# Flamingo block with a routed feed-forward layer: where four things of the opening sit in PSUM, and where the last quarter of the routing table stands in TensorE's order

## The chip, the cores and the metric

One Trainium2 chip, one core of it. The metric is the device time of one execution in microseconds (us), as the median of several runs. A traced execution has its own time, which stands beside its span below.

## What is computed

A layer of attention over a context, and a feed-forward layer with routed and shared experts, each with a layer norm before it and a gate (a hyperbolic tangent) behind it. In short:

```python
# x (4, 512, 512), ctx (4, 512, 128)
p    = layernorm(x)
kv   = ctx @ W_k.T + b_k                       # (4, 512, 128)
out  = einsum('bij,bjd->bid', p, kv)
sim  = einsum('bid,bjd->bij', out, kv) * 512 ** -0.5
attn = softmax((sim - mean) * rsqrt(var + 1e-6) * gamma + beta)
x    = x + tanh(g_xattn) * attn

h       = layernorm(x).reshape(2048, 512)
scores  = sigmoid(h @ gate_w)                  # 32 experts
top 2 of 4 groups, then the top 4 experts of these; weights made to sum to 2.5
routed  = sum over a token's 4 experts of weight * relu(h @ Wu[e]) ** 2 @ Wd[e]
shared  = relu(h @ Wsu) ** 2 @ Wsd             # inner size 1024
out     = x + tanh(g_ffn) * (routed + shared)
```

## The kernel before

It has three stages that run into one another.

The **front** takes the four batches (512 tokens each) through the attention and, behind that, three of them through the shared expert. A batch is turned on TensorE (`ctx_t`, `kv_t`, `kv_rows`, `p_t`, `out_t`), its four tiles of scores are made (`score`), ScalarE takes their squares and exponentials (`squares`, `copied`, `exps`), VectorE scales, shifts and adds them (`scaled`, `shifted`, `added`) and makes the second norm (`x2_part`, `x2_spread`, `h_norm`). The normed rows are turned on TensorE again (`h_t`, four tiles a batch), and each is split in a high part by ScalarE (`h_t` there) and a low part by VectorE (`h_low`). A product of the shared expert is three matmuls: high by high, low by high, high by low. The shared expert goes in pieces of 128 inner columns, eight a batch, numbered 0 to 23: `up_shared(g)`, then Relu and squares (`relu2(g)`), then the low part (`low_part(g)`), then `down_shared(g)`, which adds into the banks D0 to D3. Piece 0's up product goes in two halves of columns.

The **routing** begins when all logits are there. VectorE picks the experts and the places of the tokens in the experts' lists. The table that says which token sits at which place is a product of 0/1 matrices, made in four quarters by `select(q)` on TensorE in bank T0; ScalarE makes half of the left matrices (its own `select`), VectorE the other half and the right ones. Behind the last quarter one product with zeros closes the table (semaphore `pe_ix`). VectorE then reads it and writes the indices of the gather (`idx_g`), and GpSimd gathers the rows of the first tiles from memory with an indirect DMA each (`gather`). A second small table, of the experts of each tile, is turned on TensorE in T1 (`pe_tab`).

The **routed stage** runs over 81 tiles of 128 rows. For each, TensorE turns the gathered rows (`rows`), multiplies by the expert's first matrix (`up`), turns the result (`act_t`) and multiplies by the second (`down`); ScalarE and VectorE split rows, results and weights, GpSimd gathers and scatters, SyncE loads the weights of the next expert once VectorE has split those of one before. The end adds the rows up and does the shared expert of the last batch.

What sets the order: each engine's instructions stand in an order written out by hand at the end of its block and run in that order; semaphores order the engines against each other. PSUM has eight banks here: T0, T1, U0, U1, D0 to D3. Which of them holds what is said by small functions (`sim_bank`, `h_bank`, `up_bank`, `mean_bank`), and each use of a bank waits for the last reader of what was in it. On TensorE the order around the two places is, before:

```python
h_t(0, 0); h_t(0, 1); h_t(0, 2); h_t(0, 3)
up_shared(0, 0); up_shared(0, 1)
score(2, 0); score(2, 1); logits_t(0); up_shared(1); logits(0)
score(2, 2); up_shared(2); ...
...
select(2); up_shared(22); down_shared(20)
select(3); close of the table; turn of the second table
up_shared(23); down_shared(21)
rows(0); down_shared(22); rows(1); down_shared(23); up(0)
```

Line 1801 is the helper `mm`, so nearly all matmuls of the trace have that line: they are told apart by their bank and operands. L1960 is `h_t`, L1824 `ctx_t`, L1995 `logits` on TensorE; L733 is ScalarE's `h_t`, L727 its `exps`, L719 its Relu, L747 its `logits_t`, L877 and L880 its `select`; L1085 is VectorE's `x_part`, L1108 `scaled`, L1148 `h_low`, L1156 `logits`, L1174 `low_part`, L1180 `add_shared`, L1518 the end of its small tables, L1565 `tile_square`; L614 is the gather. `PEld` rows are TensorE's loads of the stationary matrix.

Of the kernel before, what the change touches and what calls it, by code (L numbers as in the profile page):

```python
# [5 lines left out]
P = 128  # L6
N_BATCH, SEQ, H = 4, 512, 512
DC = 128
TPB = SEQ // P
# [25 lines left out]
def block_kernel(nc, x, ctx_in, g_xattn, g_ffn, w_k, b_k, ln_gamma, ln_beta,  # L35
# [6 lines left out]
    with ExitStack() as stack:  # L42
# [237 lines left out]
        def sim_bank(b, it):  # L280
            return D[it] if b < 2 else T[it % 2]

# [4 lines left out]
        def h_bank(b, it):  # L287

            return U[0] if b == 0 and it == 2 else T[0] if b == 0 and it == 3 else T[it % 2]

        def up_bank(g):

            return U[0 if g else 1]

# [357 lines left out]
        def _(ac):  # L652
# [12 lines left out]
            def ctx_t(b):  # L665

                ac.wait_ge(s["pe_ctxT"], b + 1)
                ac.activation(ctxT[:, :], T[0][:, :], ACT.Copy, accum_out=csum[:, 0:1]).then_inc(s["act_ctxT"], 1)

# [382 lines left out]
        def _(ve):  # L1052
# [165 lines left out]
            score_spread(1)  # L1218
            x_part(2, 0)
            x_part(2, 1)  # L1220
            h_low(0, 0)
            h_low(0, 1)
            h_low(0, 2)
            h_low(0, 3)
            scaled(1, 0)
            shifted(1, 0)
# [291 lines left out]
            ve.tensor_scalar(done_tab[0:1, :], cntE[0:1, :], 1.0, None, ALU.add).then_inc(s["dve_tab"], 1)  # L1518
            low_part(22)

# [5 lines left out]
            nth()  # L1526
            ve.tensor_scalar(idx_g[:, :], tsum[:, :], -1.0, 0.0, ALU.add, ALU.max).then_inc(s["dve_idx"], 1)
            ve.wait_ge(s["pe_tab"], 1)
            ve.tensor_copy(tab[0:1, :], T[1][0:1, 0:2 * P]).then_inc(s["dve_tab"], 1)  # L1529
# [269 lines left out]
        def _(pe):  # L1799
# [17 lines left out]
            def ctx_t(b):  # L1817
                pe.wait_ge(d_ctx[b], 16)
                if 0 < b < 3:
                    pe.wait_ge(s["act_kv"], b)  # L1820
                elif b == 3:
                    pe.wait_ge(s["dve_hT"], TPB + 3)
                for j in range(TPB):
                    i_ = pe.transpose(T[0][:, j * P:(j + 1) * P], ctx_b[:, j, :], ident[:, :])  # L1824
                i_.then_inc(s["pe_ctxT"], 1)

            def mean(b):

                pe.wait_ge(s["act_ctxT"], b + 1)
                if b == 1:  # L1830
                    pe.wait_ge(s["act_outT"], 1)
                elif b == 2:
                    pe.wait_ge(s["act_pT"], 2 * TPB - 1)
                elif b == 3:
                    pe.wait_ge(s["dve_lg"], 1)
                mm(mean_bank(b)[:, 0:1], wkT[:, :], csum[:, 0:1]).then_inc(s["pe_mean"], 1)
# [55 lines left out]
            def score(b, it):  # L1892
                if it == 0:
                    pe.wait_ge(s["act_outT"], b + 1)
                if b == 1:
                    pe.wait_ge(s["dve_u"], it + 1)
                elif b == 2:
                    pe.wait_ge(s["dve_hT"], TPB)
                    if it >= 2:
                        pe.wait_ge(s["act_sim"], it - 1)  # L1900
                elif b == 3:
                    pe.wait_ge(s["act_pT"], TPB * b + TPB)
                    if it >= 2:
                        pe.wait_ge(s["act_sim"], TPB + it - 1)
                mm(sim_bank(b, it)[:, :], outs_of(b)[:, it * P:(it + 1) * P], keys_of(b)).then_inc(s["pe_sim"], 1)

            def up_shared(g, part=None):

                b, k = g // SB, g % SB
                if g:  # L1910
                    if part != 1:
                        pe.wait_ge(s["act_r"], g)
                elif part == 0:
                    pe.wait_ge(s["dve_ws"], 2)
                    pe.wait_ge(s["act_outT"], 3)
                if k == 0:
# [24 lines left out]
            def h_t(b, it):  # L1941
                pe.wait_ge(s["dve_h"], TPB * b + it + 1)
                if b == 0 and it >= 2:
                    if it == 2:
                        pe.wait_ge(s["act_mean"], 5)
                    else:
                        pe.wait_ge(s["dve_hT"], 1)
                elif it >= 2:
                    if b < N_BATCH - 1:
                        pe.wait_ge(s["dve_hT"], TPB * b + it - 1)  # L1950
                    else:
                        pe.wait_ge(s["act_tT"], it - 1)
                elif b == 0:
                    pe.wait_ge(s["act_pT"], 3 * TPB)
                elif b < N_BATCH - 1:
                    pe.wait_ge(s["act_sim"], TPB * (b - 1) + it + 3)
                else:
                    pe.wait_ge(s["dve_hT"], TPB * (b - 1) + it + 3)
# [4 lines left out]
            def logits_t(b):  # L1963
# [14 lines left out]
                if b == 0:  # L1978
                    pe.wait_ge(s["d_gate"], 16 * 2)
                    pe.wait_ge(s["act_r"], 1)  # L1980
                elif b == 1:
# [62 lines left out]
            up_shared(0, 1)  # L2044
            score(2, 0)
            score(2, 1)
            logits_t(0)
            up_shared(1)
# [95 lines left out]
            up_shared(22)  # L2144
            down_shared(20)
            select(3)
            mm(table, zeros[:, :], nothing, False, True).then_inc(s["pe_ix"], 1)
            pe.wait_ge(s["dve_tabT"], 1)
            for j in range(2):
# [170 lines left out]
```

## Time and profile before

| | us |
|---|---|
| median of 3 runs | 553.31 |
| lowest and highest run | 552.16, 555.45 |
| the profiled execution, its own time | 557.28 |
| its span | 555.4 |
| TensorE busy | 538.7 (97%) |
| VectorE busy | 412.7 (74%) |
| ScalarE busy | 336.2 (61%) |
| GpSimd busy | 197.7 (36%) |

The page cuts the span into 40 slices (13.9 us each) and gives the busy share of each engine in tenths. TensorE shows a 9 in all but the first, the third and the last slice, and its granted clock is at full speed throughout (2.4 GHz). VectorE shows a 9 in the four slices from 28 to 83 us. A row of a timeline reads: start, how long, engine, line, operation, output and inputs, shapes, how many in a row, and in brackets how long the engine had been idle before it and what ended that. Neighbouring rows of one engine overlap by some 0.1 to 0.2 us, since the end of an instruction is its last write; the start of the next is the better mark.

### The profile page before, as it was taken

The page shows a single profiled execution, that of the slowest core. Times are in us where ns is not written, and L with a number is a line of the kernel's source. Part 1 is how long each engine was busy: PE and PEld are TensorE (multiplying, and loading weights), DVE is VectorE, ACT ScalarE, POOL GpSimd, SP SyncE. Part 2 cuts the span into 40 slices and gives each one's busy share as a digit, 9 for nine tenths or more (in the row PEclk, how much of TensorE's full clock was granted, in tenths as well). Part 3 has the DMA queues.
Part 4 walks back from the last instruction along what each step waited for, and adds up shares of the span by engine and source line. Part 5 has one row for each costly group of instructions (what it writes and reads, how often), then busy time and mean ns, then how long its engine had stood idle before and what let it go on. Part 6 is the DMA issues. An engine that isn't in the chain of part 4 may idle for free.

```text
span 555.4 us, 11126 instructions
## 1 busy us (share of the span) xinstructions
PE 538.7 (97%) x3090; PEld 436.7 (79%) x3091; DVE 412.7 (74%) x906; ACT 336.2 (61%) x669; POOL 197.7 (36%) x194
## 2 busy tenths in 40 slices
PE   7989999999999999999999999999999999999997
PEld 5546776777888878999999888888898888897553
DVE  4799995595979948676779696775766665667997
ACT  4779573745337845677778676765766666663210
POOL 2110000000000044565667575676556655532000
PEclk9999999999999999999999999999999999999999
DMA  8930102006000037978798788687798777899997
GB/s 311 358 110 28 41 36 76 2 1 228 1 1 1 1 90 214 369 248 267 262 317 249 266 262 261 210 297 258 234 328 257 243 238 241 268 317 370 413 414 301
DMA packets 56393, 116.48 MB, mean 210 GB/s; under 512 B 5493, under 2 KB 24054, under 8 KB 55926
## 3 DMA queue, kind: packets, MB, share of 16 engines
q1 hardware_dynamic: 43200, 72.97, 39.6%
q0 software_dynamic: 12960, 42.48, 21.4%
q8 instruction: 35, 0.57, 0.4%
q14 instruction: 48, 0.39, 0.2%
q10 hardware_dynamic: 150, 0.07, 0.0%
HBM read 85.87 MB, written 29.62 MB: 208 GB/s over the span
## 4 chain that ended last, share of the span: by engine, by line
PE 73%; DVE 10%; ACT 5%; issue 4%; another core or an unknown queue 3%; DMA 1%; ACTq 1%; DVEq 0%; POOLq 0%
PE D L1801 32%; PE U L1801 31%; PE T L2162 4%; PE D L2181 2%; PE T L1801 2%; ACT xgT_hi L914 1%; DVE X L1126 1%; DVE bst L1085 1%; DVE xgT_lo L1560 1%; DVE bst L1131 1%; DVE PS L1108 1%; DVE PS L1114 1%; ACT erel L919 1%; DMA xg<-h_rows,idx_g 1%
## 5 line engine op out<-in xcount | busy, mean ns | idle before, releaser
L621 POOL DMA_INDIRECT y_rows<-yb,idx_s x81 | 95.5, 1179 | 89.0 <-ACT yb L931 62.7
L614 POOL DMA_INDIRECT xg<-h_rows,idx_g x81 | 89.8, 1108 | 103.9 <-DVE tab L1529 73.0
L1560 DVE TENSOR_TENSOR xgT_lo<-T,xgT_hi 128x512 fp32r<-128x512 f32 x81 | 55.8, 689 | 39.8 <-ACT xgT_hi L914 33.8
L931 ACT ACTIVATE yb<-D 128x512 f32<-128x512 f32 x81 | 48.8, 602 | 46.7 <-PE D L1801 37.6
L1801 PE MATMUL U<-wu_hi,xgT_hi 128*128 x324 | 59.2, 304 | 3.8 <-DVE xgT_lo L1560 3.4
L1565 DVE SCALAR_TENSOR_TENSOR eact<-U,erel 128x256 f32<-128x256 f32 x81 | 33.9, 419 | 32.7 <-issue 16.8
L1801 PE MATMUL D<-wd_hi,eaT_hi 128*128 x162 | 57.4, 435 | 0.8 <-DVE eaT_lo L1570 0.8
L919 ACT ACTIVATE erel<-U 128x256 f32<-128x256 f32 x81 | 31.0, 383 | 38.3 <-remote 19.1
L914 ACT ACTIVATE xgT_hi<-T 128x512 fp32r<-128x512 f32 x81 | 48.6, 600 | 6.1 <-issue 3.4
L1801 PE MATMUL U<-wu_lo,xgT_hi 128*128 x324 | 51.9, 282 | 0.0
L1801 PE MATMUL U<-wu_hi,xgT_lo 128*128 x324 | 51.9, 282 | 0.0
L1801 PE MATMUL D<-wd_lo,eaT_hi 128*128 x162 | 50.6, 394 | 0.0
L1801 PEld LDWEIGHTS U<-wu_hi,xgT_hi 128*128 128x128 f32 x324 | 44.5, 189 | 7.6 <-issue 7.0
L1801 PE MATMUL D<-wd_hi,eaT_lo 128*128 x162 | 50.1, 391 | 0.0
L2162 PE MATMUL T<-ident,xg 128*128 128x128 f32 x324 | 48.5, 272 | 0.8 <-DMA xg<-h_rows,idx_g 0.8
L2162 PEld LDWEIGHTS T<-ident,xg 128*128 128x128 f32 x324 | 40.1, 140 | 11.4 <-DMA xg<-h_rows,idx_g 1.2
L1550 DVE TENSOR_TENSOR wu_lo<-wu,wu_hi x32 | 39.2, 1225 | 9.2 <-issue 9.1
L1801 PEld LDWEIGHTS U<-wu_hi,xgT_lo 128*128 128x128 f32 x324 | 44.4, 190 | 0.0
L1801 PEld LDWEIGHTS U<-wu_lo,xgT_hi 128*128 128x128 f32 x324 | 44.2, 188 | 0.1
L1778 DVE SCALAR_TENSOR_TENSOR X<-yg,w,X 128x512 f32<-128x512 f32 x60 | 40.7, 747 | 4.4 <-DMA yg<-y_rows 4.3
L588 POOL TENSOR_TENSOR rstd<-veps,mhalf 128x4 f32<-128x4 f32 x8 | 8.1, 1012 | 98.0 <-DVE veps L1136 75.1
L1801 PE MATMUL D<-wsd_hi,act_hi 128*128 128x512 f32 x96 | 39.4, 410 | 0.0
(261 smaller groups left out, 1140.6 us busy)
## 6 DMA issues: line engine op xcount, KB each, us to landing
wu<-in_L_ffn_Wu SPq DMA_DIRECT2D x32, 512.0 KB
wd<-in_L_ffn_Wd SPq DMA_DIRECT2D x32, 512.0 KB
yg<-y_rows SPq DMA_DIRECT2D x18, 512.0 KB, 11.2
out<-X SPq DMA_DIRECT2D x16, 256.0 KB, 6.0
X<-in_x SPq DMA_DIRECT2D x3, 1024.0 KB, 11.5
h_rows<-HR SPq DMA_DIRECT2D x3, 1024.0 KB, 4.3
yg<-y_rows SPq DMA_DIRECT2D x3, 1024.0 KB, 11.8
wsu<-in_L_ffn_Wsu SPq DMA_DIRECT2D x2, 1024.0 KB, 8.6
```

Of the source, the lines that this page charges most:

```text
L614: pool.indirect_dma_start(out=xg[:, u, :], out_offset=None, in_=h_dram[:, :], in_offset=bass.IndirectOffsetOnAxis(ap=idx_g[:, t:t + 1], ax ...
L621: pool.indirect_dma_start(out=y_dram[:, :], in_=yb[:, u, :], in_offset=None, out_offset=bass.IndirectOffsetOnAxis(ap=idx_s[:, t:t + 1], ax ...
L914: ac.activation(xgT_hi[:, t % 2, :, :], T[t % 2][:, :].rearrange("p (h n) -> p h n", h=HB), ACT.Copy)\
L919: ac.activation(erel[:, t % 2, :], U[t % 2][:, 0:INNER], ACT.Relu)\
L931: ac.activation(yb[:, t % UNROLL, :], D[2 + t % 2][:, :], ACT.Copy)\
L1550: ve.tensor_tensor(wu_parts[1][:, ds(split_at(v), W_N)], wu2[:, ds(raw_at(v), W_N)], wu_parts[0][:, ds(split_at(v), W_N)].bitcast(f32), AL ...
L1560: ve.tensor_tensor(xgT_lo[:, t % 2, :, :], T[t % 2][:, :].rearrange("p (h n) -> p h n", h=HB), xgT_hi[:, t % 2, :, :].bitcast(f32), ALU.su ...
L1565: ve.scalar_tensor_tensor(eact[:, t % 2, :], U[t % 2][:, 0:INNER], 0.0, erel[:, t % 2, :], ALU.max, ALU.mult).then_inc(s["dve_eact"], 1)
L1778: ve.scalar_tensor_tensor(X[:, t, :], row_at(t, k), w4[:, t * TOPK + k:t * TOPK + k + 1], X[:, t, :], ALU.mult, ALU.add).then_inc(s["dve_c ...
L1801: return pe.matmul(o, l, r, start=start, stop=stop)
L2162: i_ = pe.transpose(T[t % 2][:, h * P:(h + 1) * P], xg[:, t % UNROLL, h * P:(h + 1) * P], ident[:, :])
L2181: i_ = pe.transpose(D[t % 2][:, k * P:(k + 1) * P], eact[:, t % 2, k * P:(k + 1) * P], ident[:, :])
```

## The change

Banks: the last of batch 0's four turned tiles goes to U1 (it went to T0) and the up product of piece 0 to T0 (it went to U1). Batch 2's scores take T1, T0, T1, T0 (they took T0, T1, T0, T1). Batch 3's turned context goes to U1 (it went to T0). The waits follow the banks: `h_t(0, 3)` waits for ScalarE's copy of batch 2's output and no longer for the low part of tile 0; `up_shared(0, 0)` loses its wait for that copy; `score(2, 1)` waits for the Relu of piece 0, and `logits_t(0)`, which stands ahead of it now, doesn't; `h_t(1, 0)` waits for all four copies of batch 2's scores, not three; `ctx_t(3)` waits for VectorE's first `logits` and no longer for the low part of batch 1's third tile.

Orders: VectorE does the four `h_low(0, ...)` ahead of `x_part(2, 0)` and `x_part(2, 1)`. TensorE does `logits_t(0)` ahead of `score(2, 1)`, and `select(3)` with the close of the table ahead of `down_shared(20)`. VectorE does `low_part(22)` behind the indices of the gather.

```diff
         def sim_bank(b, it):
-            return D[it] if b < 2 else T[it % 2]
+            return D[it] if b < 2 else T[(it + 1) % 2] if b == 2 else T[it % 2]
+
+        def ctx_bank(b):
+
+            return U[1] if b == N_BATCH - 1 else T[0]
...
         def h_bank(b, it):
 
-            return U[0] if b == 0 and it == 2 else T[0] if b == 0 and it == 3 else T[it % 2]
+            return U[it % 2] if b == 0 and it >= 2 else T[it % 2]
 
         def up_bank(g):
 
-            return U[0 if g else 1]
+            return U[0] if g else T[0]
...
-                ac.activation(ctxT[:, :], T[0][:, :], ACT.Copy, accum_out=csum[:, 0:1]).then_inc(s["act_ctxT"], 1)
+                ac.activation(ctxT[:, :], ctx_bank(b)[:, :], ACT.Copy, accum_out=csum[:, 0:1]).then_inc(s["act_ctxT"], 1)
...
             score_spread(1)
-            x_part(2, 0)
-            x_part(2, 1)
             h_low(0, 0)
             h_low(0, 1)
             h_low(0, 2)
             h_low(0, 3)
+            x_part(2, 0)
+            x_part(2, 1)
             scaled(1, 0)
...
             ve.tensor_scalar(done_tab[0:1, :], cntE[0:1, :], 1.0, None, ALU.add).then_inc(s["dve_tab"], 1)
-            low_part(22)
 
             ve.wait_ge(s["pe_ix"], 1)
...
             ve.tensor_scalar(idx_g[:, :], tsum[:, :], -1.0, 0.0, ALU.add, ALU.max).then_inc(s["dve_idx"], 1)
+            low_part(22)
             ve.wait_ge(s["pe_tab"], 1)
...
                 elif b == 3:
-                    pe.wait_ge(s["dve_hT"], TPB + 3)
+                    pe.wait_ge(s["dve_lg"], 1)
                 for j in range(TPB):
-                    i_ = pe.transpose(T[0][:, j * P:(j + 1) * P], ctx_b[:, j, :], ident[:, :])
+                    i_ = pe.transpose(ctx_bank(b)[:, j * P:(j + 1) * P], ctx_b[:, j, :], ident[:, :])
...
                 elif b == 2:
                     pe.wait_ge(s["act_pT"], 2 * TPB - 1)
-                elif b == 3:
-                    pe.wait_ge(s["dve_lg"], 1)
                 mm(mean_bank(b)[:, 0:1], wkT[:, :], csum[:, 0:1]).then_inc(s["pe_mean"], 1)
...
                 elif b == 2:
                     pe.wait_ge(s["dve_hT"], TPB)
-                    if it >= 2:
+                    if it == 1:
+                        pe.wait_ge(s["act_r"], 1)
+                    elif it >= 2:
                         pe.wait_ge(s["act_sim"], it - 1)
...
                 elif part == 0:
                     pe.wait_ge(s["dve_ws"], 2)
-                    pe.wait_ge(s["act_outT"], 3)
...
                     else:
-                        pe.wait_ge(s["dve_hT"], 1)
+                        pe.wait_ge(s["act_outT"], 3)
...
                 elif b < N_BATCH - 1:
-                    pe.wait_ge(s["act_sim"], TPB * (b - 1) + it + 3)
+                    pe.wait_ge(s["act_sim"], TPB if b == 1 else TPB * (b - 1) + it + 3)
...
                 if b == 0:
                     pe.wait_ge(s["d_gate"], 16 * 2)
-                    pe.wait_ge(s["act_r"], 1)
...
             score(2, 0)
+            logits_t(0)
             score(2, 1)
-            logits_t(0)
             up_shared(1)
...
             up_shared(22)
-            down_shared(20)
             select(3)
             mm(table, zeros[:, :], nothing, False, True).then_inc(s["pe_ix"], 1)
+            down_shared(20)
             pe.wait_ge(s["dve_tabT"], 1)
```

## Rows read from the trace of the kernel before

**Rows 1.** The page: busy time of the engines, share of the span, instructions

```profile
PE 538.7 (97%) x3090; PEld 436.7 (79%) x3091; DVE 412.7 (74%) x906; ACT 336.2 (61%) x669; POOL 197.7 (36%) x194
```

**Rows 2.** Busy time by stretch: length, then busy us of PE, PEld, DVE, ACT, POOL

```profile
98.00:112.00 14.00, 14.00 (x68) 11.05 (x67) 7.85 (x18) 9.71 (x21) 1.01 (x1) 1.00 0.01 2
```

**Rows 3.** Timeline of TensorE, 28 to 89 us

```profile
41.59 0.63 PE L1960 MATMUL T<-ident,HR 128*128 128x128 f32 x4 [1.51 <-DVE hT_lo L1148]
42.19 0.71 PE L1801 MATMUL U<-hT_hi,wsu_hi 128*128 128x256 f32 x4
...
45.17 1.88 PE L1801 MATMUL T<-keyT,ctxT 128*128 128x512 f32 x4
...
51.73 0.60 PE L1995 MATMUL U<-ident,lgT 128*128 128x128 f32 x4
...
53.42 1.20 PE L1801 MATMUL U<-hT_hi,wsu_hi 128*128 128x512 f32 x4 [0.23 <-ACT act L719]
...
73.86 0.63 PE L1824 MATMUL T<-ident,ctx_b 128*128 128x128 f32 x4 [0.67 <-DVE hT_lo L1148]
...
88.44 3.59 PE L1801 MATMUL U<-pT,kv 128*128 128x512 f32 x8
```

**Rows 4.** Timeline of ScalarE, 39 to 54 us

```profile
39.30 1.08 ACT L733 ACTIVATE hT_hi<-T 128x512 fp32r<-128x512 f32 x2
...
45.00 0.72 ACT L727 ACTIVATE PS<-PS,nmax 128x512 f32<-128x512 f32 x1 [0.34 <-DVE nmax L1114]
...
50.60 0.59 ACT L747 ACTIVATE lgT<-U 128x512 f32<-128x512 f32 x1
...
52.78 0.59 ACT L719 ACTIVATE act<-U 128x512 f32<-128x512 f32 x1
```

**Rows 5.** Timeline of VectorE, 39 to 88 us

```profile
39.57 1.28 DVE L1085 BATCH_NORM_STATS2 bst<-X 128x6 f32<-128x512 f32 x2
40.77 1.27 DVE L1148 TENSOR_TENSOR hT_lo<-T,hT_hi 128x512 fp32r<-128x512 f32 x2
...
43.49 0.74 DVE L1108 SCALAR_TENSOR_TENSOR PS<-D,rstd,gam 128x512 f32<-128x512 f32 x1
...
87.04 0.67 DVE L1156 TENSOR_REDUCE LG<-U 128x128 f32<-128x512 f32 x1
```

**Rows 6.** The chain that ended last, 193 to 204 us: start, length, what

```profile
193.59 2.72 PE D L1801 x12
196.31 0.87 PE T L1801 x17
...
199.39 4.26 DMA xg<-h_rows,idx_g
```

**Rows 7.** Timeline of TensorE: the first gathered rows, and tile 2's up product

```profile
203.69 0.66 PE L2162 MATMUL T<-ident,xg 128*128 128x128 f32 x4 [0.82 <-DMA xg<-h_rows,idx_g]
...
214.67 0.75 PE L1801 MATMUL U<-wu_hi,xgT_hi 128*128 x4 [0.41 <-DVE xgT_lo L1560]
```

**Rows 8.** Timeline of ScalarE: the end of its last quarter of the table

```profile
191.68 1.15 ACT L880 ACTIVATE selA<-selA,onesE 128x1024 f16<-128x1024 f16 x1
```

**Rows 9.** Timeline of VectorE, 193 to 213 us

```profile
193.37 0.16 DVE L1518 TENSOR_SCALAR done_tab<-cntE 1x32 int32<-1x32 f32 x1
...
202.15 0.69 DVE L1174 TENSOR_TENSOR act_lo<-act,act_hi 128x512 fp32r<-128x512 f32 x1 [3.36 <-ACT act L723]
...
210.35 1.41 DVE L1180 SCALAR_TENSOR_TENSOR X<-D,g_tanh,X 128x512 f32<-128x512 f32 x2 [0.25 <-PE D L1801]
212.20 0.42 DVE L1565 SCALAR_TENSOR_TENSOR eact<-U,erel 128x256 f32<-128x256 f32 x1 [0.44 <-ACT erel L919]
```

**Rows 10.** Timeline of GpSimd: the second and the third gather

```profile
200.99 1.03 POOL L614 DMA_INDIRECT xg<-h_rows,idx_g  x1 [0.31 <-issue]
202.33 1.40 POOL L614 DMA_INDIRECT xg<-h_rows,idx_g  x1 [0.30 <-issue]
```

**Rows 11.** Waits of 206 to 500 us: us in total, times, longest

```profile
ACT erel L919 <- remote: 19.1, 9, 3.0
```

## The prediction

> **What bounds the kernel now.** I read the page's busy times first: TensorE works 97% of the span, no other engine over 74% [rows 1]. So a gain must come out of the 3% in which TensorE idles, and the change removes hardly any work. Next, the busy time by stretch: from about 84 us on TensorE has no idle time in the front (the stretch of 98 to 112 us stands for all up to 196 us: 14.00 of 14.00) [rows 2], so what it wins earlier it keeps, as long as the others deliver. Then TensorE's timeline, for the brackets with idle time. In the change's reach there are four: 1.51 us ahead of the last turned tile of batch 0, 0.23 us ahead of piece 2's up product, 0.67 us ahead of batch 3's turned context [rows 3], and 0.82 us ahead of the first gathered rows [rows 7]. The first, the third and the fourth are what the edits aim at. Whether each pays is read from who is last next.
>
> **Part 1, batch 0's turned tiles (28 to 54 us): worth nothing.** `h_t(0, 3)` waited for the low part of tile 0, since both had T0. TensorE had been free since 41.59 - 1.51 = 40.08 us [rows 3]. In U1 the tile waits for ScalarE's copy of batch 2's output, which ScalarE has behind it when it begins with the turned tiles at 39.30 us [rows 4], so it starts at 40.1, 1.5 us earlier. What follows is VectorE's. A high part on ScalarE takes some 0.6 us (the pair 1.08), so tile 0's is done at 39.9 [rows 4]. VectorE is free from 39.57 us, where `x_part(2, 0)` began, and does one of these steps in (40.77 - 39.57) / 2 = 0.60 us [rows 5]. In the new order it waits until 39.9, does four low parts to 42.3 and the two `x_part` to 43.5. `scaled(1, 0)` began at 43.49 before [rows 5]. VectorE trades one small wait for another and is where it was.
>
> TensorE does get ahead. The first half of piece 0's up product may start when the second low part is done, 39.9 + 1.27 = 41.2 us, and the two halves took 45.17 - 42.19 = 2.98 us [rows 3], so they end at 44.2 and not 45.17: a lead of 0.9 to 1.0 us. The second half needs the fourth low part, 39.9 + 1.8 + 0.7 = 42.4, which is in time. From there to `logits(0)` stands 51.73 - 45.17 = 6.56 us of TensorE work, whose sum the new order leaves alone, so it arrives at about 50.8. There it meets ScalarE. Its exponential of 45.00 us waited for VectorE [rows 4], which has not moved, and from there to 55 us ScalarE's timeline shows no gap. Its copy of the logits ends at 50.60 + 0.59 = 51.19, so the lead shrinks to 0.5; its Relu of piece 1 ends at 52.78 + 0.59 = 53.37, and piece 2's up product begins at 53.42 as before [rows 3, 4]. The lead is gone. The wait that the change adds, `score(2, 1)` for the Relu of piece 0, stands ahead of `up_shared(1)` and all behind it on TensorE. The Relu comes right behind that exponential: 45.00 + 0.7 + 0.6 = 46.3 us [rows 4]. Of the 6.56 us, 2.98 are piece 1's up product; of the other 3.58, all but one score (1.88 / 2 = 0.9) stand ahead of `score(2, 1)` now, so TensorE comes to it at 44.2 + 2.6 = 46.8: it costs nothing, with 0.5 us of cover. `h_t(1, 0)`, which now waits for the fourth copy of scores, waits anyway for batch 1's norm, and that stands in VectorE's order behind all of batch 1's softmax. Bounds for part 1: nothing on the low side; on the high side the lead, 1.0 us, and at the very most the whole idle time, 1.51 us. I take nothing, since the 0.23 us bracket at 53.42 [rows 3] shows who is last there.
>
> **Part 2, batch 3's context (74 us): 0.67 us.** `ctx_t(3)` waited 0.67 us for a low part on VectorE [rows 3]. In U1 it waits for VectorE's first `logits`, long past, so it starts when piece 2's down product ends, at 73.19. Late next could be three things. `kv_t(3)` still waits for the next low part (0.6 us more), but half an up product of 1.5 us stands between. ScalarE's copy and mean wait only for the context and move with it. And `out_t(3)` at 88.44 overwrites U1 and waits for VectorE's `logits(1)`, done at 87.04 + 0.67 = 87.71 [rows 3, 5]: a slack of 0.73, of which 0.67 is used up. It holds, barely. From there TensorE has no idle time and its feeders wait for it, so I count 0.67 us in full; bounds 0 and 0.67.
>
> **Part 3, the table (193 to 215 us): 0.69 us.** Before, `down_shared(20)` ran from 193.59 to 196.31 (2.72 us), the quarter and the close to 197.18 [rows 6]. Then came indices, issue and flight of the gather: 199.39 - 197.18 = 2.21, and 4.26 us [rows 6], in all 6.47 us. TensorE covered 203.69 - 0.82 - 197.18 = 5.69 of them, and idled 0.82 [rows 7]. Now the down product stands behind the close and covers as well: 5.69 + 2.72 = 8.41 against 6.47, 1.9 us to spare. The 0.82 us go. Can the quarter run that early? ScalarE has its part at 191.68 + 1.15 = 192.83 [rows 8], TensorE comes at 193.59: 0.76 to spare. VectorE is through its small tables at 193.53 [rows 9], and the table closes at 194.46. `low_part(22)` waits behind the indices; if it stood ahead, it would hold them for ScalarE's squares. Behind it wait only the copy of the second table, which TensorE turns behind the same down product as before, and `down_shared(22)`, which comes after the first rows. Behind `down_shared(20)`, nobody waits for it sooner than piece 23.
>
> What is late next is VectorE. It idles 0.25 us ahead of `add_shared` at 210.35 and 0.44 us ahead of `tile_square` at 212.20 [rows 9], both for TensorE, and tile 2's up product waits for it at 214.67 [rows 7]. It can move forward by 0.25 + 0.44 = 0.69 us and no more, so 0.69 of the 0.82 arrive. GpSimd's queue: the four gathers come 2.7 us earlier relative to TensorE, and it then waits for the second index as before. Bounds: 0.44 (if the first of the two stays) and 0.82.
>
> A third gather took 1.40 us and the second 1.03 us [rows 10]; beside the third ran a `low_part` of 0.69 us that starts at 202.15 [rows 9]. The first gather now has `low_part(22)` beside it. The Trainium skill, SBUF — State Buffer, Who interferes with whom, says that a VectorE instruction with two inputs in SBUF contends with a GpSimd instruction that reads SBUF, and that the loser stands still for the whole instruction. By the row that is 0.37 us a gather, by the rule up to 0.69; either is within the 1.9 us. It speaks against the reordering, and I put it into the chance of the third rival below, not into the sum.
>
> **Sum.** 0 + 0.67 + 0.69 = 1.36 us, 0.25%. The profiled execution took 557.28 us and would take 555.92. It lies 3.97 us above the median of 553.31; I carry the difference over: 553.31 - 1.36 = 551.95, rounded to 551.9.
>
> **Rivals.** (a) TensorE's lead of part 1 is kept, because ScalarE or VectorE move forward after all: another 1.0 us, 551.0, at most 1.51, 550.4. For it: a 1.5 us wait is really taken away. Against it: the 0.23 us bracket and the sum on VectorE. (b) Part 2 is taken back at `out_t(3)`, where 0.06 us is left, or by the next norm: only part 3 stays, 552.6. (c) The gather isn't earlier than TensorE needs it, because something else holds it (GpSimd also waits for twenty down products and for the small tables, or contention): only part 2 stays, 552.6. Against it: both conditions hold before 194 us. (d) Slower: weights in the routed stage. ScalarE waits there nine times for SyncE's word that weights have landed, 19.1 us in all, 2.1 us each, 3.0 the longest [rows 11]. Most of that is hidden behind TensorE. If earlier tiles bring one more of the mean size onto TensorE's path, 551.95 + 2.1 = 554.1, slower than before; from two on, 556.2, it is slower by over 0.5%. It decides as soon as the landings shift by more than the 1.36 us won. Against it: VectorE's splits ask for the weights, and these move forward with the tiles.
>
> **Chances.** The forecast 0.52, (a) 0.15, (b) 0.12, (c) 0.07, (d) 0.14. A measurement of this kernel can tell about 0.5%, 2.8 us, from no change, since its runs lie 3.3 us apart. Faster by more than that (below 550.5) needs the far end of (a), 0.05, or the scatter of the runs upon the forecast and (a), 0.11: 0.16. Slower by more (above 556.1) is the second half of (d), 0.07. Within: 0.77. The range reaches from 549.8, (a)'s end less scatter, to 554.8, (d) with one wait and scatter.
>
> **What would show it.** The trace after should have `ctx_t(3)` without its bracket; piece 2's up product at about 53.4 us with a short wait for the Relu (right), or a us earlier (rival a); a wait ahead of `out_t(3)` (rival b); the first gather about 2.2 us behind the close, the rows' turn without a bracket, and tile 2's up product some 1.4 us earlier than 214.67, at 213.3. If that holds and the end doesn't move, the brackets of the routed stage have grown (rival d). The forecast is wrong if TensorE waits for ScalarE at the last quarter or at `score(2, 1)`.

## The result, and the profile after

| | before | after |
|---|---|---|
| median, 22 runs each | 556.11 us | 554.62 us |
| mean of the same runs | 556.28 | 554.18 |
| the profiled execution, its own time | 557.28 | 555.18 |
| its span | 555.4 | 553.3 |

The ratio is 0.996, with a 95% interval of 0.9943 to 0.9978: the change makes the kernel faster by 1.2 to 3.2 us of 556, about 2.2, which is inside the 0.5% that was called no change. It was forecast as 1.36 us, or 0.9975. The forecast time of 551.9 us was too low by 2.7 us, nearly all of it for a reason that has nothing to do with the change: it started from the median of three runs, 553.31, and the median of 22 runs of the same kernel is 556.11.

The page of after, the span and the busy times, for rows 1:

```profile
span 553.3 us, 11125 instructions
...
PE 538.4 (97%) x3090; PEld 436.4 (79%) x3091; DVE 411.9 (74%) x906; ACT 337.0 (61%) x669; POOL 197.1 (36%) x194
```

TensorE does the same work (538.4 us against 538.7) in 2.1 us less. Lines moved by two to four: mm is L1805 now, `h_t` L1963, `logits` L1997, `ctx_t` L1828, VectorE's `h_low` L1152, its `logits` L1160, `low_part` L1178. Traces don't begin at the same point of the work: VectorE's first `h_norm` starts at 37.05 us in the trace of before, at 36.67 in that of after, and anywhere from 36.13 to 37.73 in the thirteen traces of this text. So all shifts from here on are taken with the start of that `h_norm` as the zero.

The timeline of TensorE after, 39 to 88 us, for rows 3:

```profile
39.10 1.04 PE L1963 MATMUL U<-ident,HR 128*128 128x128 f32 x8
40.98 0.71 PE L1805 MATMUL T<-hT_hi,wsu_hi 128*128 128x256 f32 x4 [0.84 <-DVE hT_lo L1152]
...
43.93 1.02 PE L1805 MATMUL T<-keyT,ctxT 128*128 128x512 f32 x2
...
46.74 1.12 PE L1805 MATMUL T<-keyT,ctxT 128*128 128x512 f32 x2
...
50.88 0.66 PE L1997 MATMUL U<-ident,lgT 128*128 128x128 f32 x4 [0.26 <-ACT lgT L751]
...
53.06 1.19 PE L1805 MATMUL U<-hT_hi,wsu_hi 128*128 128x512 f32 x4 [0.51 <-ACT act L723]
...
65.33 1.11 PE L1963 MATMUL T<-ident,HR 128*128 128x128 f32 x8 [0.19 <-DVE HR L1147]
...
72.68 0.60 PE L1828 MATMUL U<-ident,ctx_b 128*128 128x128 f32 x4
```

The bracket of 1.51 us is gone, and three stand in its place: 0.84 us ahead of piece 0's up product, 0.26 ahead of the turned logits, 0.51 ahead of piece 2's up product. `score(2, 0)` begins at 43.93, 0.86 us earlier by the zero; piece 2's up product at 53.06, 0.02 us later. The lead was there and was given back. At `ctx_t(3)` there is no bracket any more: 72.68 against 73.86 is 0.80 us earlier by the zero.

Why VectorE is where it was, its timeline from 39 us on, for rows 5:

```profile
39.55 1.29 DVE L1152 TENSOR_TENSOR hT_lo<-T,hT_hi 128x512 fp32r<-128x512 f32 x2 [0.27 <-ACT hT_hi L737]
40.75 1.28 DVE L1152 TENSOR_TENSOR hT_lo<-U,hT_hi 128x512 fp32r<-128x512 f32 x2
41.95 1.28 DVE L1089 BATCH_NORM_STATS2 bst<-X 128x6 f32<-128x512 f32 x2
43.14 0.73 DVE L1112 SCALAR_TENSOR_TENSOR PS<-D,rstd,gam 128x512 f32<-128x512 f32 x1
...
86.40 0.67 DVE L1160 TENSOR_REDUCE LG<-U 128x128 f32<-128x512 f32 x1
```

It waits 0.27 us in one place where it waited in another, does the same six steps, and comes to `scaled(1, 0)` at 43.14, which by the zero is 0.03 us later than 43.49. The timeline of ScalarE after, for rows 4:

```profile
38.92 1.08 ACT L737 ACTIVATE hT_hi<-T 128x512 fp32r<-128x512 f32 x2
...
44.64 0.72 ACT L731 ACTIVATE PS<-PS,nmax 128x512 f32<-128x512 f32 x1 [1.87 <-DVE nmax L1118]
...
50.25 0.58 ACT L751 ACTIVATE lgT<-U 128x512 f32<-128x512 f32 x1
...
52.42 0.59 ACT L723 ACTIVATE act<-U 128x512 f32<-128x512 f32 x1
```

Its wait for VectorE grew from 0.34 to 1.87 us. Before, it had also waited 1.38 us for the fourth turned tile, in its timeline of before:

```profile
42.26 0.60 ACT L733 ACTIVATE hT_hi<-T 128x512 fp32r<-128x512 f32 x1 [1.38 <-PE T L1960]
```

Now it has this tile sooner, and what it waited in two places it waits in one. From 44.64 on ScalarE has no gap until the Relu of piece 1 has been done, at 53.01, and TensorE is bound to that.

The table, for rows 6 to 10, first in the timeline of TensorE after:

```profile
192.33 0.85 PE L1805 MATMUL T<-selB,selA 128*128 128x96 f16 x16
193.02 0.33 PE L1805 MATMUL T<-zeros 128*128 128x384 f16 x1
195.94 0.38 PE L2152 MATMUL T<-ident,eid 128*1 128x128 f32 x2
...
201.62 0.60 PE L2164 MATMUL T<-ident,xg 128*128 128x128 f32 x4
...
212.74 0.75 PE L1805 MATMUL U<-wu_hi,xgT_hi 128*128 x4 [0.59 <-DVE xgT_lo L1564]
```

ScalarE's last step for the table, in its timeline after:

```profile
190.57 1.15 ACT L884 ACTIVATE selA<-selA,onesE 128x1024 f16<-128x1024 f16 x1
```

VectorE, its timeline after over the same stretch:

```profile
193.38 0.56 DVE L1526 TENSOR_REDUCE tsum<-T 128x96 f32<-128x384 f32 x1 [0.95 <-PE T L1805]
...
194.56 0.68 DVE L1178 TENSOR_TENSOR act_lo<-act,act_hi 128x512 fp32r<-128x512 f32 x1
...
208.36 0.68 DVE L1564 TENSOR_TENSOR xgT_lo<-T,xgT_hi 128x512 fp32r<-128x512 f32 x1
208.96 1.40 DVE L1184 SCALAR_TENSOR_TENSOR X<-D,g_tanh,X 128x512 f32<-128x512 f32 x2
210.28 0.41 DVE L1569 SCALAR_TENSOR_TENSOR eact<-U,erel 128x256 f32<-128x256 f32 x1
```

GpSimd, its timeline after, with the first three gathers:

```profile
195.57 1.30 POOL L618 DMA_INDIRECT xg<-h_rows,idx_g  x1 [70.31 <-DVE idx_g L1530]
197.17 1.03 POOL L618 DMA_INDIRECT xg<-h_rows,idx_g  x1 [0.31 <-issue]
198.50 1.01 POOL L618 DMA_INDIRECT xg<-h_rows,idx_g  x1 [0.30 <-issue]
```

The quarter runs straight behind piece 22's up product; ScalarE's part was ready at 191.72, 0.6 us ahead. The first gather starts 2.2 us behind the close, as before, and the first rows are turned without a bracket. VectorE now goes through `add_shared` and `tile_square` without one, and tile 2's up product waits for it still, 0.59 us. By the zero it starts 1.55 us earlier.

### The profile page after: what moved, and what is told of

Same layout as the page of the kernel before. It is cut to its first block, busy times and chain, and to the rows that moved or that the text cites. A ratio compares the mean times of both kernels' runs of the same rounds, so it can differ in the third digit from the quotient of the medians.

```text
span 553.3 us, 11125 instructions
## 1 busy us (share of the span) xinstructions
PE 538.4 (97%) x3090; PEld 436.4 (79%) x3091; DVE 411.9 (74%) x906; ACT 337.0 (61%) x669; POOL 197.1 (36%) x194
## 4 chain that ended last, share of the span: by engine, by line
PE 76%; DVE 8%; ACT 6%; issue 4%; another core or an unknown queue 3%; ACTq 1%; DMA 1%; DVEq 1%
PE U L1805 32%; PE D L1805 32%; PE T L2164 4%; PE D L2183 2%; PE T L1805 2%; ACT xgT_hi L918 1%; PE T L1963 1%; DVE xgT_lo L1564 1%; DVE X L1130 1%; ACTq L353 1%; DVE bst L1135 1%; DVE PS L1118 1%; ACT erel L923 1%; DVE bst L1089 1%
## 5 line engine op out<-in xcount | busy, mean ns | idle before, releaser
L1805 PE MATMUL U<-wu_hi,xgT_hi 128*128 x324 | 59.3, 304 | 3.0 <-DVE xgT_lo L1564 2.5
L1805 PE MATMUL D<-wd_hi,eaT_hi 128*128 x162 | 57.4, 435 | 0.9 <-DVE eaT_lo L1574 0.6
L1805 PE MATMUL U<-wu_hi,xgT_lo 128*128 x324 | 51.9, 283 | 0.0
L1805 PE MATMUL U<-wu_lo,xgT_hi 128*128 x324 | 51.8, 282 | 0.0
L1805 PE MATMUL D<-wd_lo,eaT_hi 128*128 x162 | 50.6, 393 | 0.0
L1805 PE MATMUL D<-wd_hi,eaT_lo 128*128 x162 | 50.2, 391 | 0.0
L1805 PEld LDWEIGHTS U<-wu_hi,xgT_hi 128*128 128x128 f32 x324 | 44.5, 189 | 6.5 <-issue 5.9
L1805 PEld LDWEIGHTS U<-wu_hi,xgT_lo 128*128 128x128 f32 x324 | 44.4, 190 | 0.0
L1805 PEld LDWEIGHTS U<-wu_lo,xgT_hi 128*128 128x128 f32 x324 | 44.2, 188 | 0.0
L1805 PE MATMUL D<-wsd_hi,act_hi 128*128 128x512 f32 x96 | 39.5, 412 | 0.0
```

The source lines that it names most:

```text
L1805: return pe.matmul(o, l, r, start=start, stop=stop)
```

## The experiments

Their traces are read by the same marks. Each entry is the shift against the first trace of before in us, by the zero; the stage is the time from the fifth tile's rows to the first up product of the last batch's shared expert. The same kernels came on three chips, A, B and C; for the first traces of before and after the chip isn't recorded.

| kernel | piece 2's up | h_t(1, 0) | ctx_t(3) | out_t(3) | rows(0) | tile 2's up | 5th tile's rows | stage | chip |
|---|---|---|---|---|---|---|---|---|---|
| before | 0 | 0 | 0 | 0 | 0 | 0 | 0 | 284.1 | |
| before again, b0 | 0.01 | 0.01 | 0.01 | 0.00 | 0.13 | 0.16 | 0.17 | 283.9 | B |
| after | 0.02 | 0.02 | -0.80 | -0.76 | -1.69 | -1.55 | -1.54 | 283.2 | |
| after again, a0 | 0.03 | 0.03 | -0.75 | -0.75 | -1.71 | -1.57 | -1.56 | 282.8 | B |
| after, third, a1 | 0.04 | 0.04 | -0.82 | -0.74 | -1.70 | -1.56 | -1.55 | 277.9 | C |
| table alone, e1 | 0.00 | -0.01 | -0.01 | -0.02 | -0.98 | -0.83 | -0.83 | 273.3 | A |
| context alone, e2 | 0.00 | 0.00 | -0.82 | -0.77 | -0.64 | -0.63 | -0.64 | 273.3 | A |
| turned tiles alone, e3 | 0.04 | 0.03 | 0.02 | 0.03 | 0.06 | 0.08 | 0.09 | 273.3 | A |
| low_part(22) back, e4 | 0.02 | 0.03 | -0.83 | -0.75 | -1.71 | -1.57 | -1.56 | 273.3 | A |
| high_part(3) early, e5 | -1.67 | -0.43 | -1.25 | -1.21 | -2.12 | -1.98 | -1.96 | 284.1 | B |
| and x_part late, e6 | -1.69 | -1.61 | -1.65 | -1.20 | -2.13 | -1.99 | -1.95 | 284.0 | B |
| after, tile 2 early, e7 | 0.01 | 0.01 | -0.82 | -0.77 | -1.73 | -2.40 | -2.10 | 276.4 | C |
| all four, e9 | -1.67 | -1.60 | -2.42 | -1.79 | -2.75 | -3.41 | -3.13 | 277.5 | C |

The front repeats itself to some 0.1 us (`ctx_t(3)` of the changed kernel stands at 0.75 to 0.82 in three traces), and up to 0.17 behind the first gather of before, whose landing varies: the bracket there is 0.82, 0.94, 0.84 and 0.94 us in the four traces with the old order of the table (before, b0, e3, e2). So marks tell apart what the time of a run can't, since runs of one kernel lie up to 7 us apart. For the same reason the own times of the kernels that ran once decide nothing: on chip A 545.15 (e1), 545.25 (e2), 547.19 (e3) and 545.31 (e4) beside 546.07 for before, one run too; on chip B 556.33 (e5) and 554.36 (e6) beside a median of 557.29.

**The table alone (e1_table).** The kernel before with these two orders:

```diff
             up_shared(22)
-            down_shared(20)
             select(3)
             mm(table, zeros[:, :], nothing, False, True).then_inc(s["pe_ix"], 1)
+            down_shared(20)
...
-            low_part(22)
             ve.wait_ge(s["pe_ix"], 1)
...
+            low_part(22)
             ve.wait_ge(s["pe_tab"], 1)
```

> The kernel before with the table's reordering alone (select(3) and the close ahead of down_shared(20), low_part(22) behind the indices). All shifts are against before, with VectorE's first h_norm as the zero. Forecast of the prediction: nothing moves up to ctx_t(3) (its 0.67 us bracket stays); the bracket of 0.82 us at the first gathered rows is gone; rows(0) 0.8 us earlier, tile 2's up product 0.7 us earlier. Rival (c), something else holds the gather: rows(0) keeps a bracket and moves by less than 0.4 us. If the two parts of the change need one another: less than 0.7 here, and more in the whole change than the sum of the parts.

Measured: nothing moves up to `out_t(3)`, the first rows are turned 0.98 us earlier, tile 2's up product 0.83. Two rows of its timeline of TensorE:

```profile
202.21 0.60 PE L2162 MATMUL T<-ident,xg 128*128 128x128 f32 x4
...
213.34 0.75 PE L1801 MATMUL U<-wu_hi,xgT_hi 128*128 x4 [0.60 <-DVE xgT_lo L1560]
```

Nothing else held the gather; rival (c) is out. The edit gives 0.16 us more at the first rows than the bracket of 0.82.

**The context alone (e2_context).** The kernel before with `ctx_bank`, its use in both engines, and the wait for `dve_lg`:

```diff
                 elif b == 3:
-                    pe.wait_ge(s["dve_hT"], TPB + 3)
+                    pe.wait_ge(s["dve_lg"], 1)
                 for j in range(TPB):
-                    i_ = pe.transpose(T[0][:, j * P:(j + 1) * P], ctx_b[:, j, :], ident[:, :])
+                    i_ = pe.transpose(ctx_bank(b)[:, j * P:(j + 1) * P], ctx_b[:, j, :], ident[:, :])
```

> The kernel before with ctx_t(3) in U1 alone. Same zero. Forecast: ctx_t(3) begins 0.7 to 0.8 us earlier, out_t(3) too, and TensorE keeps it to the first gathered rows, where the bracket of 0.82 us stays (GpSimd and the indices move along). Tile 2's up product 0.7 to 0.8 us earlier. Rival (b), it is taken back at out_t(3) or at the next norm: the shift is below 0.3 us at the rows(0).

Measured: 0.82 us at `ctx_t(3)`, 0.77 at `out_t(3)`, 0.64 at the first rows, where the bracket is back, a little longer, in its timeline of TensorE:

```profile
202.50 0.66 PE L2164 MATMUL T<-ident,xg 128*128 128x128 f32 x4 [0.94 <-DMA xg<-h_rows,idx_g]
```

Nothing is taken back on the way, rival (b) is out as well; the last 0.12 us are the gather's flight, which varies. At tile 2's up product the two alone make 0.63 + 0.83 = 1.46 us, and both together gave 1.55 to 1.57: with the table's new order TensorE no longer waits for that flight.

**The turned tiles alone (e3_turned).** All of the change but the context's bank and the table's order. Two of its banks:

```diff
-            return U[0] if b == 0 and it == 2 else T[0] if b == 0 and it == 3 else T[it % 2]
+            return U[it % 2] if b == 0 and it >= 2 else T[it % 2]
...
-            return U[0 if g else 1]
+            return U[0] if g else T[0]
```

> The kernel before with the banks and orders of batch 0's turned tiles, piece 0 and batch 2's scores alone (ctx_t(3) stays in T0, the table's order stays). Same zero. Forecast, part 1 is worth nothing: TensorE comes to score(2, 0) some 0.9 us earlier, and piece 2's up product, h_t(1, 0) and all behind them stand within 0.1 us of before. Rival (a), the lead is kept: they stand 0.5 to 1.0 us earlier.

Measured: `score(2, 0)` 0.86 us earlier, piece 2's up product 0.04 us later, and nothing behind it earlier. The largest part of the diff is worth nothing by itself.

**low_part(22) back ahead of the table's reading (e4_low22).** The changed kernel with that one line moved back.

> The changed kernel with low_part(22) put back ahead of the reading of the table. VectorE then waits for ScalarE's second square of piece 22 (ends at 194.4 us in the changed kernel's trace), so the indices and the first gather come 1.7 us later than in the changed kernel. Forecast from the slack of 1.9 us that the prediction worked out: rows(0) still has no bracket or one below 0.1 us, and tile 2's up product stands where it stands in the changed kernel. If the slack is smaller than reckoned, a bracket of up to 1 us is back, and the place of low_part(22) is what the gain of the table hangs on.

Measured: VectorE waits 2.04 us for ScalarE's squares, the sum over the table starts at 195.77 and the first gather at 197.95, which by the zero is 1.67 us later than in the changed kernel, and the first rows are turned where they were, without a bracket. Its timeline of VectorE:

```profile
195.16 0.69 DVE L1178 TENSOR_TENSOR act_lo<-act,act_hi 128x512 fp32r<-128x512 f32 x1 [2.04 <-ACT act L727]
195.77 0.55 DVE L1527 TENSOR_REDUCE tsum<-T 128x96 f32<-128x384 f32 x1
```

So of the slack of 1.9 us at least 1.67 are there, and the move of `low_part(22)` isn't what the gain hangs on; the earlier close of the table, ahead of `down_shared(20)`, is.

**The kernel before and the changed kernel again (b0_before, a0_after, a1_after).**

> The kernel before, unchanged, traced again beside the others. On the first chip its routed stage (from the fifth tile's rows to the shared expert's tail) took 284.1 us, with some 12 us of waits in it; the four experiments so far ran on another chip and had 273.3 us each. If that is the chip and not the edits, this run has about 273.3 us on that chip too. The front's shifts against the first trace of before should be within 0.05 us.

> The changed kernel again, timed. Forecast: TensorE at tile 2's up product 1.55 us earlier than before with VectorE's first h_norm as zero, the routed stage as long as before's on the same chip, so 1.4 to 1.7 us faster in all, 0.997. If the 2.2 us of the first comparison (ratio 0.996) hold part of a shorter routed stage, its ratio is nearer to 0.996 on a chip whose routed stage waits, and 0.997 on one whose doesn't.

> The changed kernel once more, timed, on whatever chip comes. Forecast: the front's marks as in the two traces so far (tile 2's up product 1.55 us earlier than before, VectorE's first h_norm as zero). If the 0.9 us by which the timed gains (2.2 and 2.8 us) pass the front's 1.6 belong to the routed stage of a chip whose stage waits, a chip with a short stage (273 us) gives 1.4 to 1.8 us; if they are the change's everywhere, over 2 us.

Measured: before's stage took 283.9 us on chip B. No trace of before was taken on chip A, but its one run there took 546.07 us where it takes 557.3 on B, so the 273.3 us of the four experiments are the chip's and not the edits'. The marks of before agree within 0.02 us up to `out_t(3)`, and differ by 0.13 to 0.17 behind the gather, more than the 0.05 expected. The changed kernel on chip B: 0.995 (0.9932 to 0.9967), means 557.2 and 554.6. On chip C: 0.9963 (0.9941 to 0.9985), means 550.8 and 548.6. That chip's stage is the middle one, not the short one that the expectation spoke of, so the two outcomes that it set against each other stay undecided. Over the three comparisons the means differ by 2.1, 2.6 and 2.2 us, more than the 1.4 to 1.7 expected.

**What the lead of the turned tiles was lost to (e5_high3).** The changed kernel with ScalarE's second split of the down weights in the 1.87 us gap:

```diff
             high_part(2)
+            high_part(3)
             exps(1, 0)
             relu2(0)
-            high_part(3)
```

> The changed kernel with ScalarE's high_part(3) ahead of exps(1, 0), in the 1.87 us in which ScalarE waits for VectorE. It takes away what the lead of part 1 was lost to: ScalarE's order between 45 and 53 us. Forecast, if ScalarE is who was last at piece 2's up product: that product starts 1.2 to 1.5 us earlier than in the changed kernel; TensorE then waits over 1 us at h_t(1, 0) for VectorE's norm, which gains only the 0.37 us that VectorE waited for high_part(3); so from there on 0.3 to 0.4 us are left. Rival: the lead is kept in full, 0.9 us or more at h_t(1, 0).

Measured: piece 2's up product 1.69 us earlier than in the changed kernel, so ScalarE's order was what held it. At `h_t(1, 0)` TensorE waits for VectorE's norm, and 0.45 us are left, and 0.4 from there to the end of the marks. Its timeline of TensorE:

```profile
51.80 1.48 PE L1805 MATMUL U<-hT_hi,wsu_hi 128*128 128x512 f32 x4
...
59.01 1.19 PE L1805 MATMUL U<-hT_hi,wsu_hi 128*128 128x512 f32 x4 [0.28 <-ACT act L723]
...
65.31 1.11 PE L1963 MATMUL T<-ident,HR 128*128 128x128 f32 x8 [0.57 <-DVE HR L1147]
```

The wait at `h_t(1, 0)` was expected above 1 us and is 0.57: another 0.28 stands ahead of piece 3's up product, and more between single matmuls (four in 1.48 us where they took 1.19).

**And VectorE's sum taken down (e6_xlate).** The same, with two `x_part` (1.2 us) fewer ahead of the norm that TensorE waits for. The expectation says that (2, 0) and (2, 1) go behind `h_norm(1)`; in the edit they go just ahead of it, and (2, 2) and (2, 3) go behind it:

```diff
             h_low(0, 3)
-            x_part(2, 0)
-            x_part(2, 1)
             scaled(1, 0)
...
+            x_part(2, 0)
+            x_part(2, 1)
+            h_norm(1)
             x_part(2, 2)
             x_part(2, 3)
-            h_norm(1)
...
+            logits(1)
             added(2, 3)
             x2_part(2, 3)
-            logits(1)
```

> e5 with two of VectorE's x_part of batch 2 (1.2 us) moved from ahead of scaled(1, 0) to behind h_norm(1), and its logits(1) ahead of added(2, 3). It takes away the second bound, VectorE's sum of work up to the norm of batch 1. Forecast: h_t(1, 0) 1.4 to 1.6 us earlier than in the changed kernel, with a wait below 0.3 us; of that about 1.1 us are left at the first gathered rows, since kv_t(3) then waits some 0.4 us for the low part of batch 1's last tile. Tile 2's up product 1.0 to 1.2 us earlier than in the changed kernel. Rival: TensorE is held elsewhere before 200 us, and less than 0.5 us is left.

Measured: `h_t(1, 0)` 1.63 us earlier than in the changed kernel, as expected. But the lead shrinks to 0.4 us, not 1.1, and all marks from the first rows on are those of the step before. Its timeline of TensorE says where:

```profile
67.49 1.22 PE L1963 MATMUL T<-ident,HR 128*128 128x128 f32 x8 [0.44 <-DVE hT_lo L1152]
...
76.11 0.66 PE L1852 MATMUL T<-ident,keyT 128*128 128x128 f32 x4 [0.28 <-ACT keyT L689]
```

The expectation had named a wait at `kv_t(3)`; the waits are at `h_t(1, 2)`, which overwrites T0 while VectorE does the postponed work first, and at `kv_rows(3)`, behind ScalarE's exponential.

**Tile 2's rows first (e7_tile2).** The changed kernel, with

```diff
             tile_square(0)
+            tile_in(2)
             add_shared(N_BATCH - 2, (2, 3))
```

and without that step in the first turn of the loop.

> The changed kernel with VectorE's low part of tile 2's rows ahead of the second pair of add_shared. It takes away what the prediction named as late next behind the table: the 0.6 us bracket ahead of tile 2's up product. Forecast: the bracket is gone, tile 2's up product and the fifth tile's rows 0.5 to 0.6 us earlier than in the changed kernel; the down product of tile 0, which waits for that add_shared, comes 1.7 us behind it and doesn't wait. Rival: tile 0's or tile 1's step waits for the later add_shared or tile_square, and less than 0.2 us is left.

Measured: the bracket of 0.6 us is gone. Tile 2's up product comes 0.84 us earlier, the fifth tile's rows 0.55; the first down product waits for VectorE's low part of tile 0's result, which now stands behind the later `add_shared` (it ends at 214.46 us, and the product starts at 214.59). The time was 0.9954 (0.9928 to 0.9979) of before on chip C, where the changed kernel had 0.9963 (0.9941 to 0.9985); these two times don't tell the kernels apart, the marks do.

**All four (e9_best).** The last but one, with `tile_in(2)` as above and what held TensorE taken away:

```diff
             h_norm(1)
             x_part(2, 2)
-            x_part(2, 3)
-            low_part(3)
-            x_spread(2)
             h_low(1, 0)
             h_low(1, 1)
+            x_part(2, 3)
+            low_part(3)
+            x_spread(2)
...
-            exps(2, 1)
             kv_t(3)
+            exps(2, 1)
```

> e6 with what held TensorE there taken away too: VectorE does h_low(1, 0) and (1, 1) ahead of x_part(2, 3), low_part(3) and the spread (TensorE waited 0.44 us for the first of them at h_t(1, 2)), ScalarE does its kv_t(3) ahead of exps(2, 1) (0.28 us at kv_rows(3)); and with e7's edit. Forecast if these two were all: the 1.6 us of lead at h_t(1, 0) reach the first gathered rows, and with e7's 0.55 tile 2's up product is 2.0 to 2.2 us earlier than in the changed kernel, 3.6 to 3.7 earlier than before; timed 0.993 to 0.994 of before. If each bound taken away shows another close behind it, as in the two steps before, 1.0 to 1.5 us are left.

Measured: 0.9929 (0.9903 to 0.9956) of before; median 547.17 us, against 548.8 of the changed kernel and 550.96 of before on the same chip. It has the lowest ratio to before of all that were timed. By the marks it is 3.13 us ahead of before at the fifth tile's rows, 1.58 ahead of the changed kernel. One bracket is left between 43 and 200 us, in its timeline of TensorE:

```profile
74.39 0.38 PE L1807 MATMUL U<-csum,wkT 128*128 128x1 f32 x2 [0.26 <-ACT ctxT L672]
```

Of the 1.6 us at `h_t(1, 0)`, 1.05 reach the gather, the lower of the two outcomes that were expected; tile 2's up product is 1.85 us earlier than in the changed kernel, where 2.0 to 2.2 were forecast.

## Why the prediction was right, and where not

**What bounds the kernel** held. All of the gain that the marks show came out of TensorE's idle time, and each wait was worth what the next in line left of it.

**Part 1, nothing,** held step for step: the lead (0.9 to 1.0 forecast, 0.86 measured), VectorE's sum (43.5 forecast against 43.49; 0.03 us later), the loss at ScalarE's copy of the logits and at the Relu. The turned tiles alone gave 0.04 us, and moving one ScalarE step moved piece 2's up product by 1.69 us, which shows who held it. The cover at `score(2, 1)` held: it began at 46.74, and the Relu (45.37 + 0.58) had ended at 45.95, 0.79 us of cover where 0.5 was reckoned.

**Part 2, 0.67 us,** was mis-sized: 0.74 to 0.82 measured, above the bound of 0.67 too. A bracket counts from the end of the row ahead, and rows that follow one another overlap: the matmuls are 0.39 us long and start every 0.23. The starts tell what a wait costs. TensorE, the matmul ahead of `ctx_t(3)` in its timeline of before, then in that of after:

```profile
72.81 0.39 PE L1801 MATMUL D<-wsd_hi,act_lo 128*128 128x512 f32 x1
```

```profile
72.44 0.39 PE L1805 MATMUL D<-wsd_hi,act_lo 128*128 128x512 f32 x1
```

From this start to that of `ctx_t(3)` it is 73.86 - 72.81 = 1.05 us before and 72.68 - 72.44 = 0.24 after: 0.81 for a bracket of 0.67. At the gather the same two distances are 1.20 (202.49 to 203.69) and 0.23 us (201.39 to 201.62): 0.97 for a bracket of 0.82, and 0.98 was measured at the first rows. So each of these brackets was worth some 0.15 us more than it says, the length of the overlap, and the trace of before had that in it.

That part 2 arrived in full is in part luck. The slack at `out_t(3)` was put at 0.73 - 0.67 = 0.06 us. With the 0.76 us that arrived there it would have been short by 0.03, but what was left is 87.30 - 86.40 - 0.67 = 0.23, since VectorE moved forward by 0.26 us too, which the prediction didn't see: its `added(2, 1)` waits for an exponential that came earlier.

**Part 3, 0.69 us,** came out at 0.75 in the whole change and 0.83 alone. The reason held: VectorE's two brackets went, TensorE's bracket for VectorE at tile 2's up product stayed, and moving VectorE's step took it away. The size is the overlap again, at VectorE: from the low part of tile 1's rows to that of tile 2's its starts are 213.85 - 209.41 = 4.44 us apart before and 211.93 - 208.36 = 3.57 after, so two brackets of 0.69 together were worth 0.87, and "0.69 us and no more" was too strict. The conditions held: ScalarE's quarter was 0.61 us ahead (0.76 forecast), VectorE's tables 0.9 as forecast, and of the 1.9 for the gather at least 1.67 were there. The contention weighed with the Trainium skill, SBUF — State Buffer, Who interferes with whom, didn't touch the first gather: `low_part(22)` ended at 195.24 and the first gather began at 195.57. That gather takes 1.30 us with no `low_part` beside it, so its length says nothing for the rule. The third gather does bear on it: it takes 1.40 to 1.41 us in the four traces with the old order, where `low_part(23)` and a second instruction with two inputs in SBUF run beside it, and 1.01 to 1.02 in after, a0, a1 and e1, where VectorE is idle meanwhile. The direction is that of the rule; the 0.39 us are less than the whole 0.69 of the `low_part`, part of which had run when the gather began.

**The sum,** 1.36, was to be 1.55 by the marks (1.56, 1.55 in the other two traces), 0.2 short for the two reasons above. The timed means say 2.1, 2.6 and 2.2 us; the intervals reach down to 1.2, 1.8 and 0.8. So 0.5 to 1.1 us of the timed gain isn't accounted for by the marks, and on chip B the 1.56 lie below the interval. In the traces the stage of the changed kernel is 0.9 us shorter than before's, and 1.1 on chip B, but the two kernels built upon it have 284.1 and 284.0 there, like before. Nor is the end the place: from the shared expert's tail to the end of the span it is 53.5 us before and 54.2 after. The 2.1 us between the two traced spans are 0.38 ahead of the zero, 1.54 in the marks and 0.87 in the stage, less 0.7 at the end; of these only the 1.54 repeat within 0.02 us in the other two traces. Whether the change shortens the routed stage a little or these executions scattered that way stays open.

**Rival (d)** named the right place for the wrong question. The stage is long where ScalarE waits for landed weights, and that is what differs between the chips, as the waits of before, of after and of the table alone show (engine, line, waited for: us in total, times, longest). Of before:

```profile
ACT erel L919 <- remote: 19.1, 9, 3.0
```

Of after:

```profile
ACT erel L923 <- remote: 15.3, 8, 2.9
```

No run here moved the loads by themselves, so this is read from the traces and not tried. On chip A, in the trace of the table alone, there is no such wait, and the stage has TensorE busy without a gap (the busy times by stretch: the stretch, its length, PE, PEld, DVE, ACT and POOL busy, granted clock, DMA share, GB/s):

```profile
216.00:488.00 272.00, 272.00 (x1880) 248.03 (x1878) 195.93 (x329) 196.90 (x383) 164.71 (x151) 1.00 0.85 280
```

But the tiles' earlier start didn't lengthen these waits (19.1 us before, 15.3 after), as the prediction's argument against the rival had it.

**The carried time** was the largest error in microseconds: the median of three runs was taken as the kernel's time. It lay 2.8 us below that of 22 runs, twice the forecast gain, while the profiled execution (557.28) lay only 1.2 above it. That the measured 554.62 us still lies in the range of 549.8 to 554.8, by 0.2 us, is luck: its upper end was put there for rival (d), which didn't happen.

## What to carry to other kernels

Before a wait is taken away by using another bank, follow the next two waits of the same engine: the 1.5 us bracket was the largest in the front and worth nothing, since two other engines stood at the end of full queues, while the one of 0.67 us paid in full, since TensorE had no other wait for 100 us behind it, and the one of 0.82 gave 0.98 at the first rows and 0.83 ten us on, where VectorE was next. Take the size of a wait from start to start and not from the bracket, which left out 0.15 us of each of these. Where a lead is lost, look for an engine ahead of it that waits (ScalarE 1.87 us in one piece here): it has the room for a step of the work that holds the lead up. Where a change is worth less than runs scatter, read marks in the trace from a common zero; they repeat to 0.1 us here, the times to some us.

## What the runs showed of the hardware

The routed stage takes 273.3 us on one chip, 276 to 278 on a second and 283 to 284 on a third, in kernels that differ only ahead of it or at its first tiles, with a mean granted clock of 0.998 to 1.000 in all; the front's marks up to `out_t(3)` agree within 0.1 us between kernels that are alike there, whatever the chip. What differs is when weights land: ScalarE's waits for them in the relus of the tiles come to 18.9 us in b0 on chip B and to nothing in e1 on chip A. Where they fall repeats too. A tile takes TensorE 3.47 us mostly. The longer ones (3.7 us and more) begin at 315, 319, 337, 348 and 359 us in both traces of before, within 0.5 us of each other (for the first the chip isn't recorded), and on chip C, in a1, e7 and e9, the first come only at 410, 418, 428, 440 and 447 us, within 0.8 us of each other. So they look like noise between chips and like structure on one.
